# Six of sixteen states scanned into SBUF, their products with C on GpSimd and their last state kept by ScalarE

## The reference

```
dt = softplus(dt_low @ dt_proj_w.T + dt_proj_b)          # per token, 512 channels
A = -exp(A_log)                                          # 512 channels x 16 states
def step(h, inp):                                        # over the tokens of a sequence
    dt_t, B_t, C_t, u_t = inp
    dA = exp(dt_t[..., None] * A)
    h = h * dA + (dt_t * u_t)[..., None] * B_t[:, None, :]
    y = einsum('bes,bs->be', h, C_t)                     # sum over the 16 states
    return h, y
y = ys + x_conv * D
y = y * silu(z)
return y @ out_proj_w.T
```

## Time and profile before

| | us |
|---|---|
| median of 3 runs | 2444.34 (2442.5 to 2446.28) |
| the profiled execution | 2433.91 |
| its span | 2432.2 |
| busy PE | 1906.7 (78%) |
| busy DVE | 1736.6 (71%) |
| busy POOL | 1200.0 (49%) |
| busy ACT | 961.4 (40%) |

### The profile page before, as it was taken

The page is one execution under the profiler, slowest core; times in us unless marked ns, Lnnn a source line. Parts: engine busy times, 40 slices in busy tenths (PEclk is TensorE's granted clock), DMA queues, the critical chain, the costliest instruction groups (busy, mean ns, idle before and its releaser), DMA issues. The chain is left out here.

```text
span 2432.2 us, 32142 instructions
## 1 busy us (share of the span) xinstructions
PE 1906.7 (78%) x9388; PEld 1330.8 (55%) x9389; DVE 1736.6 (71%) x2540; ACT 961.4 (40%) x1474; POOL 1200.0 (49%) x879
## 2 busy tenths in 40 slices
PE   4388989972796988879898888977755478989970
PEld 4288989971232434344343434433335378989970
DVE  5754656654698989889898888989926745656644
ACT  2322323321455565555555455554411422333320
POOL 1334444452466656556565556666501344545441
PEclk8588999986798999999999999998985689999995
DMA  6422222214333333333333333334303222222216
GB/s 222 156 69 72 67 84 70 79 48 151 109 130 124 122 122 123 119 113 121 121 122 114 111 121 118 128 115 128 117 1 104 69 75 71 79 73 81 79 40 210
DMA packets 147177, 254.00 MB, mean 104 GB/s; under 512 B 17567, under 2 KB 66720, under 8 KB 145472
## 3 DMA queue, kind: packets, MB, share of 16 engines
q1 hardware_dynamic: 127424, 211.36, 26.7%
q0 software_dynamic: 15360, 36.34, 5.2%
q10 hardware_dynamic: 4224, 4.19, 0.5%
HBM read 214.98 MB, written 42.47 MB: 106 GB/s over the span
## 5 line engine op out<-in xcount | busy, mean ns | idle before, releaser
L1214 POOL TENSOR_TENSOR m_dB<-m_DTU,m_BC 128x1024 f32<-128x1024 f32 x256 | 602.8, 2357 | 397.9 <-DVE PS L1330 397.6
L1330 DVE TENSOR_TENSOR_SCAN PS<-PS,m_ST,m_dB 128x512 f32<-128x512 f32 x512 | 631.2, 1279 | 99.0 <-ACT PS L1043 32.4
L1035 PE MATMUL PS<-m_G,keep_ident 128*128 128x512 f32 x1024 | 522.1, 636 | 140.8 <-DVE m_G L1340 140.4
L1043 ACT ACTIVATE PS<-m_DT,m_A 128x512 f32<-128x512 f32 x512 | 346.6, 688 | 318.3 <-DVE PS L1330 314.2
L1035 PEld LDWEIGHTS PS<-m_G,keep_ident 128*128 128x128 f32 x1024 | 191.2, 198 | 418.4 <-DVE m_G L1340 240.0
L1340 DVE TENSOR_TENSOR m_G<-PS,m_BC 128x1024 f32<-128x1024 f32 x256 | 313.3, 1224 | 21.8
L581 PE MATMUL PS<-e_xh,e_wh 128*128 128x256 f32 x1008 | 300.9, 299 | 0.0
L581 PE MATMUL PS<-e_xl,e_wh 128*128 128x256 f32 x1008 | 294.5, 292 | 0.0
L581 PE MATMUL PS<-e_xh,e_wl 128*128 128x256 f32 x1008 | 294.3, 292 | 0.0
L599 PE MATMUL PS<-e_wh,e_hh 128*128 128x256 f32 x1008 | 286.1, 284 | 3.2 <-DVE e_ysb L707 3.0
L599 PE MATMUL PS<-e_wh,e_hl 128*128 128x256 f32 x1008 | 285.3, 283 | 0.0
(11 more groups left out here) (192 smaller groups left out, 2789.6 us busy)
## 6 DMA issues: line engine op xcount, KB each, us to landing
m_BC<-bc_rows SPq DMA_DIRECT2D x512, 256.0 KB, 3.3
layer_raw<-w SPq DMA_DIRECT2D x64, 512.0 KB, 3.8
xrows<-r_xn SPq DMA_DIRECT2D x16, 512.0 KB, 3.4
yrows<-r_zrow SPq DMA_DIRECT2D x8, 1024.0 KB, 17.1
c_got<-yrows SPq DMA_DIRECT2D x16, 512.0 KB, 9.0
keep_X<-x SPq DMA_DIRECT2D x4, 1024.0 KB, 9.4
m_G<-yrows SPq DMA_DIRECT2D x8, 512.0 KB, 5.0
m_dB<-yrows SPq DMA_DIRECT2D x8, 512.0 KB, 4.9
```

The costliest lines, as they stand in the source:

```text
L1035: last = M(PS[:, B_Y + j, :], C["ident"][:, :], G[:, s % 2, j, :], start=False, stop=(s == DS - 1))
L1043: return nc.scalar.activation(out, in_, func, **kw)
L1214: G_.tensor_tensor(dB[:, s % 2, :, :], DTU[:, es, :], BC[:, s % NBC, 0:1, :].to_broadcast([P, 2, CT]), ALU.mult).then_inc(dB_ok, 1)
L1330: V.tensor_tensor_scan(PS[:, B_H + j, :], PS[:, B_DA + j, :], dB[:, s % 2, j, :], ST[:, s, e:e + 1], ALU.mult, ALU.add).then_inc(scanned, 1)
```

## The change

A new buffer HS of 128 x 2 x 512 in SBUF takes the scans of states 0, 2, 5, 8, 10 and 13 of each pair, so of 12 of the 32 states of a chunk. For these, DVE issues only the two scans; before them it waits until POOL and ACT have read HS for the previous such state (`gp_ok`, `kept_hs`). POOL forms the product (`weigh`), and issues it behind dB of the state two further on. ACT copies the last column (`keep`), behind the decay of the next state. PE and SP wait for the product of a state through `product`, which gives the semaphore and count of the engine that forms it. The other 20 states stay as they were. `fmask` is one column longer.

```diff
+        HS = sb("HS", [P, 2, CT])
...
+        S_POOL = (0, 2, 5, 8, 10, 13)
+        ON_GP = [n for n in range(STEPS) if n % DS in S_POOL]
+        ON_V = [n for n in range(STEPS) if n % DS not in S_POOL]
+
+        def product(k, n):
+            if n < 0:
+                return product(k - 1, n + STEPS)
+            if n in ON_GP:
+                return gp_ok, k * len(ON_GP) + (ON_GP.index(n) + 1)
+            return g_ok, k * len(ON_V) + (ON_V.index(n) + 1)
...
(sp)
-                        sp.wait_ge(used, k * STEPS + (n - NBC + 1))
+                        if j == 0:
+                            sp.wait_ge(dB_ok, k * STEPS + (n - NBC + 1))
+                        else:
+                            sp.wait_ge(*product(k, n - NBC))
...
(pe)
-                        pe.wait_ge(g_ok, k * STEPS + (n + 1))
+                        pe.wait_ge(*product(k, n))
...
(act)
+            def keep(k, p, s):
+                F(ST[:, s, 2 * p:2 * p + 2], HS[:, :, CT - 1], ACT.Copy, scale=fmask[:, bass.ds(k + 1, 1)]).then_inc(kept_hs, 1)
...
+                        if n in ON_GP:
+                            keep(k, p, s)
                         items(ON_ACT, n, k, par, has_front, has_back, front, back)
...
(pool)
+            def weigh(k, n):
+                s = n % DS
+                gp.wait_ge(c_in[s % NBC], k * (16 * STEPS // NBC) + 16 * (n // NBC + 1))
+                gp.wait_ge(scanned, k * (2 * STEPS) + (2 * n + 2))
+                if not (is_first(k) and n < 2):
+                    gp.wait_ge(g_read, k * STEPS + (n - 1))
+                G_.tensor_tensor(G[:, s % 2, :, :], HS[:, :, :], BC[:, s % NBC, 1:2, :].to_broadcast([P, 2, CT]),
+                                 ALU.mult).then_inc(gp_ok, 1)
...
+                        if n - 2 in ON_GP:
+                            weigh(k, n - 2)
                         items(ON_POOL, n, k, par, has_front, has_back, front, back)
...
(dve)
-                        if not (is_first(k) and n == 0):
-                            dve.wait_ge(kept, k * STEPS + n)
+                        on_gp = n in ON_GP
+                        if on_gp:
+                            so_far = k * len(ON_GP) + ON_GP.index(n)
+                            if not (is_first(k) and n == ON_GP[0]):
+                                dve.wait_ge(gp_ok, so_far)
+                                dve.wait_ge(kept_hs, so_far)
+                        else:
+                            so_far = k * len(ON_V) + ON_V.index(n)
+                            if not (is_first(k) and n == ON_V[0]):
+                                dve.wait_ge(kept, so_far)
...
-                            V.tensor_tensor_scan(PS[:, B_H + j, :], PS[:, B_DA + j, :], dB[:, s % 2, j, :], ST[:, s, e:e + 1],
+                            state = HS[:, j, :] if on_gp else PS[:, B_H + j, :]
+                            V.tensor_tensor_scan(state, PS[:, B_DA + j, :], dB[:, s % 2, j, :], ST[:, s, e:e + 1],
...
+                        if not on_gp:
                             (wait for C, the scans and g_read, product L1340, kept state L1343, as before)
```

More of the change, by code:

```diff
@@ L796, in mamba @@
         mask = sb("mask", [P, MCH + 1], U32)
-        fmask = sb("fmask", [P, MCH])
+        fmask = sb("fmask", [P, MCH + 1])
         st = sb("st", [P, 2 * CTT, 6])
@@ L832, in mamba @@
         dA_ok, dB_ok, scanned, g_ok, g_read, kept = (sem(n) for n in ("dA_ok", "dB_ok", "scanned", "g_ok", "g_read", "kept"))
+        gp_ok, kept_hs = sem("gp_ok"), sem("kept_hs")
         yz_ok, xn_ok, sq_ok, v_ok, rs_ok, hr_ok, q_ok, xa_ok = (sem(n) for n in (
@@ L932, in load @@
                 n = p * DS + s
-                for j, landed, used in ((0, b_in, dB_ok), (1, c_in, g_ok)):
+                for j, landed in ((0, b_in), (1, c_in)):
                     if n >= NBC or not is_first(k):
-                        sp.wait_ge(used, k * STEPS + (n - NBC + 1))
+                        if j == 0:
+                            sp.wait_ge(dB_ok, k * STEPS + (n - NBC + 1))
+                        else:
+                            sp.wait_ge(*product(k, n - NBC))
                     src = bc_dram[bass.ds(k, 1), j, s:s + 1, :].rearrange("o q t -> (o q) t")
@@ L1335, in turn @@
                             gated(k - 1, 1, 1 - par)
[L1336 to L1344, removed]
+                        if not on_gp:
+                            dve.wait_ge(c_in[s % NBC], k * (16 * STEPS // NBC) + 16 * (n // NBC + 1))
+                            dve.wait_ge(scanned, k * (2 * STEPS) + (2 * n + 2))
+                            if not (is_first(k) and n < 2):
+                                dve.wait_ge(g_read, k * STEPS + (n - 1))
+                            V.tensor_tensor(G[:, s % 2, :, :], PS[:, B_H:B_H + 2, :], BC[:, s % NBC, 1:2, :].to_broadcast([P, 2, CT]),
+                                            ALU.mult).then_inc(g_ok, 1)
+                            V.tensor_tensor(ST[:, s, 2 * p:2 * p + 2].bitcast(U32), PS[:, B_H:B_H + 2, CT - 1].bitcast(U32),
+                                            mask[:, bass.ds(k + 1, 1)].to_broadcast([P, 2]), ALU.bitwise_and).then_inc(kept, 1)
                         items(ON_DVE, n, k, par, has_front, has_back, None, back)
```

## The result

The changed kernel takes 2522.6 us (median of four, 2516.1 to 2532.2) against 2443.4 for the kernel before (median of four, 2442.2 to 2446.3): 1.033 times as long, 95% interval 1.0309 to 1.0351, which is 79 us more. The forecast was 2501, 57 us more. The profiled execution took 2523.4.

A forecast was written before the change was run, and what follows sets the result against it. It took DVE to set the pace in one part of the state loop and in-order PE in another. Middle, first and last chunks gave 6 x 10.3 + 3 - 8 = +57 us on 2444.3: 2501, range 2445 to 2540.

The forecast's parts named there:

- The middle chunks: Six middle chunks of the state loop: each 10.3 us slower, from products reaching PE late and its slow clock.
- the signs of being right: Trace after: PE idle for POOL at states 5, 13, 26; clock below 0.96; middle chunks 150 to 154 us.
- the walk through the chunk: One middle chunk state by state: slip 6.9 at state 5, 8.7 by 20, 12.9 at 26, +10.3 us in sum.
- the list of products: One middle chunk's twelve moved products against PE's old times: 5.0 us late at state 5, 28 together.
- the gaps of PE at states 6 to 10: Middle chunk: PE gaps of 0.2, 0.5 and 0.5 us absorb 1.2 of the slip.
- First chunk: No back items give PE some slack: +6 to the silu block, then 3 given back, so +3 us.
- Last chunk: No projections, DVE sets the pace after state 5: nine moved products save time, -8 us.
- the pj additions: Last chunk: about 6 us taken off what the nine moved products save.
- Costs put at nothing: SBUF scan 1.27 us as before, ScalarE's copy of 0.2 to 0.3 hidden, HS waits free in middle chunks.
- (2): Slower still: POOL shuts out DVE's `v` and scan 7, 16 us more, SBUF scan 10 more: 2527; chance 0.12.
- (3): Only states 5 and 26 cost, the rest is regained: +13 us, 2457; chance 0.10.
- (1): Faster: slips don't add up because scans run ahead; -122 us gives 2322, half way 2383; chance 0.16.

The follow-up runs named there:

- weigh_first: Changed kernel with POOL forming the product of state n ahead of dB(n+2) instead of behind it: 2457.8 us.
- pe_no_wait: Changed kernel with POOL's products written to an unread tile and PE adding a constant tile in their place without waiting: 2413.8 us.
- no5: Changed kernel with state 5 given back to DVE, eleven moved products a chunk left: 2509.5 us.
- late_items: Changed kernel with POOL's add and du moved from states 5 and 6 to 8 and 9, and from 27 and 28 to 28 and 30: 2509.9 us.
- dve_from_sbuf: Changed kernel with the twelve products formed by DVE from two SBUF tiles instead of by POOL; SBUF scans and ScalarE's copy stay: 2511.0 us.
- before_late: Kernel before, no product moved, with only POOL's add and du put at states 8, 9, 28 and 30: 2429.2 us.
- first_and_late: Changed kernel with product n ahead of dB(n+2) and POOL's add and du at states 8, 9, 28, 30; all twelve products moved: 2445.0 us.
- five_first_late: Changed kernel with product n ahead of dB(n+2), add and du later, and only states 18, 21, 24, 26, 29 moved: 2427.4 us.
- three_first_late: Changed kernel with product n ahead of dB(n+2), add and du later, and only states 24, 26, 29 moved: 2427.2 us.

## Why the prediction was right, and which terms were off

**The mechanism held.** PE idles at states 5, 13 and 26 released by POOL (4.88 at state 5, forecast 5.1; 1.60 at 13, forecast 2.3; 2.32 at 26, forecast 4.3), the clock falls behind state 5, and what hangs on it slips: the y sum of 5 by 5.7, the next x projection by 7.6, the `gated` of state 16 by 9.3 (the forecast had 8.7 by state 20). The middle chunks took 152 us each and their granted clock was 0.94, as the signs of being right had it. Two waits as large as that at 13 were not charged in the walk through the chunk, though the list of products had them late: PE also idles 1.68 for POOL at state 18 and 2.23 at 24. And the gaps of PE at states 6 to 10 that were to absorb 1.2 could not: the earlier trace rows leaves PE 0.75 idle in the whole 64.5 us. That the middle chunk comes out so close therefore owes something to terms that cancel. weigh_first and pe_no_wait show the lateness to be the cause, the first by removing most of it at equal work, the second by removing only the wait.

**The middle chunks were well sized:** +60 in the table, forecast 6 x 10.3 = 62. As forecast, nearly all of it lies in the first halves. The bridge between them, that the second half keeps what the first lost, held on average (+0.7 a chunk, forecast +1.6), though single halves vary by -1.4 to +3.7.

**The end chunks were mis-sized,** and that is the whole difference. First chunk: +15 where the prediction put +3. It took the missing back items for slack, but product 5 is as late there (PE idle 5.55). Timeline of after, chunk 0:

```profile
695.22 3.78 PE L1052 MATMUL PS<-m_G,keep_ident 128*128 128x512 f32 x4 [5.55 <-POOL m_G L1234]
...
701.45 0.60 ACT L1060 ACTIVATE m_XI<-PS 128x512 f32<-128x512 f32 x1 [9.87 <-PE PS L998]
```

That is 9.87 where a middle chunk has 8.02. Last chunk: +8 where it put -8. What DVE could save there was about right: without PE's wait the chunk sinks by 9.1 (pe_no_wait). But the prediction let DVE set the pace there and, beyond about 6 at the pj additions, charged nothing for PE:

```profile
1754.10 7.54 PE L1052 MATMUL PS<-m_G,keep_ident 128*128 128x512 f32 x12 [7.48 <-POOL m_G L1234]
1766.53 6.43 PE L1052 MATMUL PS<-m_G,keep_ident 128*128 128x512 f32 x8 [4.89 <-POOL m_G L1234]
```

PE idles 7.48 and 4.89, and the eight records behind the second take 0.80 us each instead of 0.47 (granted clock 0.57 from 1766 to 1773, near the lower level). By the steps of the sum: middle chunks 2 below forecast, first chunk 12 and last chunk 16 above. That makes the 26 between the loop's +83 and the forecast's +57; by the medians (+79) it is 22.

**Costs put at nothing:** the scan into SBUF takes 1268 ns against 1277 into PSUM in the same kernel (forecast 1.27); the copy on ScalarE 0.28; DVE's wait for HS never over 1.0 us in pe_no_wait, nor over 1.2 in no5; POOL's product 2354 (forecast 2.35). DVE's work fell by 138 (forecast 132; the small `v` alone fell from 12 to 3 in all eight chunks), POOL's rose by 221 (226).

**The rivals.** (2), where `v` is shut out by POOL: it did not come. `v` takes 0.30 at 1145.93 (2.00 in the earlier trace rows), and ends as one POOL instruction hands over to the next at 1146.2. It could have come: in late_items `v` takes 2.32 in the six middle chunks and in no5 2.0, and scan 7 starts behind it. That it takes 0.30 here is a matter of where it falls between POOL's instructions, which the forecast did not work out, so that leaving it out was partly luck. The lock is real, as dve_from_sbuf shows, but it did not carry the loss of the changed kernel. (3), only 5 and 26 cost: no5 takes state 5 away and gives back 13, since state 8 takes its place. (1), faster: even without PE's wait for POOL the kernel was only 29 below the one before (pe_no_wait, 2413.8), far above 2322 or 2383, with DVE waiting for ScalarE's decays.

**Left open:** why the clock drops at state 19 in before_late and at 20 in before; how much of what no5 and late_items keep is product 8 and how much `v`; how much of the loss in dve_from_sbuf is DVE's time in the lock and how much the later product and dB, and what the last 16 us of first_and_late over before_late are. The fastest versions (five_first_late, before_late, three_first_late; 2427 to 2429) beat both kernels and can't be told apart.

## What to carry to other kernels

When work moves from a busy engine to an idle one, don't go by the busy shares: compare the time at which its result exists with the time at which the next in-order consumer takes it. Here products that come late for PE (at state 5, 7.3 us after the scan instead of 1.3) cost more than the 138 us taken off DVE could bring. Place the moved instruction ahead of whatever has slack in its new queue. And before a gain is credited to an edit, run what was reordered along with it alone. Here the reordering gave the whole gain, and against it the twelve moved products still cost 16 us.

## What the runs showed of the hardware

Unexpected: an elementwise product on DVE with both inputs in SBUF, beside a busy POOL, costs 2.61 us on average instead of the 1.23 that one PSUM input costs, and slows POOL's dB from 2357 to 2481 ns on average (dve_from_sbuf). Without a POOL instruction beside it, it costs 1.22. A small DVE instruction gets in where two POOL instructions without a pause meet (`v`: 0.30 us in the changed kernel, 2.32 in late_items, where it comes just behind the start of one), so a full POOL queue held it up for one instruction at most. And moving four POOL instructions by one to three states, with no other edit, is worth 0.56% of this kernel.
